# Graph attention's edge pass: source rows gathered per segment instead of per work item

## The reference, cut to what matters

```python
h = (x @ W.T).reshape(n, H, D)                      # one row per node
h_src, h_dst = h[src], h[dst]                       # 200000 edges, sorted by dst
alpha = einsum(h_src, a_src) + einsum(h_dst, a_dst)
alpha = alpha + sum(relu(edge_attr @ edge_W.T + edge_b) * h_dst, -1)
alpha = where(alpha >= 0, alpha, 0.2 * alpha)
ex = exp(alpha - segment_max(alpha, dst)[dst])
attn = ex / segment_sum(ex, dst)[dst]
out = segment_sum(h_src * attn, dst)
```

## Time and profile before

| | us |
|---|---|
| median of 3 runs | 4161.73 (4161.46 to 4166.39) |
| the profiled execution | 4158.91 |
| its span, first to last instruction | 4157.1 |
| PE / DVE / ACT / POOL busy | 3517.1 / 2547.6 / 2043.5 / 2185.5 |

### The profile page before, as it was taken

One profiled execution on the slowest core, in us unless ns is written; L12 is line 12 of the kernel. 1 busy time (PEld: TensorE's weight loads), 2 busy tenths in 40 slices (PEclk: granted clock), 3 DMA queues, 4 the chain that ended last, 5 costly groups with the idle time before them and its releaser, 6 DMA issues.

```text
span 4157.1 us, 87425 instructions
## 1 busy us (share of the span) xinstructions
PE 3517.1 (85%) x22054; PEld 2416.0 (58%) x22055; DVE 2547.6 (61%) x6056; ACT 2043.5 (49%) x5653; POOL 2185.5 (53%) x2124
## 2 busy tenths in 40 slices
PE   4788899958888888888888888888888869919999
PEld 3447788835555555555555555555555547808888
DVE  5657655557777777777777777777777754411121
ACT  2312333326666666666666666666666644503232
POOL 3302000047777777777777777777777711151111
PEclk8899999989999999999999999999999989959999
DMA  4631011145555555555555555555555531021110
GB/s 151 199 124 48 28 35 32 33 100 125 135 134 139 136 134 138 136 139 138 138 136 141 141 141 144 140 140 139 138 143 139 143 140 30 27 63 36 34 39 25
DMA packets 352296, 449.23 MB, mean 108 GB/s; under 512 B 170970, under 2 KB 275163, under 8 KB 350456
## 3 DMA queue, kind: packets, MB, share of 16 engines
q0 software_dynamic: 95568, 267.78, 25.6%
q10 hardware_dynamic: 108338, 124.27, 9.8%
q1 hardware_dynamic: 147943, 52.09, 5.2%
HBM read 389.57 MB, written 55.13 MB: 107 GB/s over the span
## 4 chain that ended last, share of the span: by engine, by line
PE 34%; DMA 17%; issue 13%; SPq 13%; POOL 8%; DVE 7%; ACT 4%; ACTq 3%; POOLq 0%; DVEq 0%
SPq L428 9%; DMA al<-h_tab,idx 6%; DMA al<-pen_d 6%; PE bank L1175 5%; PE bank L1187 5%; PE bank L989 4%; POOL al L521 4%; PE bank L1134 4%; PE bank L998 4%; PE bank L1083 3%; SPq L414 3%; PE bank L1024 2%; DMA gbuf<-h_tab,idx 2%; POOL gbuf L521 2%; PE bank L902 1%
## 5 line engine op out<-in xcount | busy, mean ns | idle before, releaser
L521 POOL DMA_INDIRECT al<-h_tab,idx x976 | 1107.1, 1134 | 309.9 <-issue 279.9
L521 POOL DMA_INDIRECT gbuf<-h_tab,idx x784 | 843.5, 1076 | 400.3 <-issue 379.8
L1024 PE MATMUL bank<-oneh_t,hbt 125*128 125x512 bf16 x2640 | 719.7, 413 | 189.0 <-DVE oneh_t L1442 167.4
L746 ACT ACTIVATE enc<-bank,eb 128x512 f32<-128x512 f32 x880 | 554.7, 682 | 299.6 <-issue 192.5
L1449 DVE SCALAR_TENSOR_TENSOR prod<-enc,adst,bank 128x512 f32<-128x512 f32 x880 | 628.6, 734 | 11.9 <-PE bank L1014 11.9
L1083 PE MATMUL bank<-msg,oneh 128*125 128x264 f32 x2352 | 629.2, 414 | 7.3 <-DVE r L1536 3.9
L1083 PEld LDWEIGHTS bank<-msg,oneh 128*125 128x125 f32 x2352 | 473.2, 205 | 160.4 <-issue 47.3
L1024 PEld LDWEIGHTS bank<-oneh_t,hbt 125*128 x2640 | 245.6, 102 | 529.3 <-issue 353.4
L763 ACT ACTIVATE dist<-iota_n,dtile 128x125 f32<-128x125 f32 x1760 | 552.7, 389 | 0.7 <-PE bank L1083 0.5
L1046 PE MATMUL bank<-prod,hsel 128*32 128x128 f32 x7040 | 283.8, 279 | 58.6 <-issue 58.3
L1536 DVE TENSOR_TENSOR r<-r,bank 125x264 f32 x440 | 187.3, 426 | 221.7 <-PE bank L1014 195.1
(11 more groups left out here) (254 smaller groups left out, 5599.7 us busy)
## 6 DMA issues: line engine op xcount, KB each, us to landing
dstb<-dst ACTq DMA_DIRECT2D x440, 125.0 KB
al<-pen_d SPq DMA_DIRECT2D x1760, 4.0 KB
att<-attrx ACTq DMA_DIRECT2D x880, 24.0 KB
al<-h_tab,idx POOLq DMA_INDIRECT x976
link<-links SPq DMA_DIRECT2D x880, 0.2 KB
gbuf<-h_tab,idx POOLq DMA_INDIRECT x784
attrx<-al ACTq DMA_DIRECT2D x8, 1176.0 KB, 12.3
hsplit<-hb POOLq DMA_DIRECT2D x25, 375.0 KB, 5.5
```

What stands on the lines that cost most here:

```text
L521: pool.indirect_dma_start(slot(n)[:, c, :], None, h_tab, bass.IndirectOffsetOnAxis(ap=idx[g % 2][:, k:k + 1], axis=0)).then_inc(gathered[n ...
L746: m = act.activation(enc[n % 2][:, k, :], bank[k][:, :], ACT.Relu, bias=eb[:, k:k + 1])
L1024: pe.matmul(bank[2 + 2 * q + k][:, :], hbt[:, ds(t & (HT - 1), 1), a, k * 128:(k + 1) * 128].rearrange("p t c -> p (t c)"), oneh_t[q][:, : ...
```

## The change

Gathers are counted by segments. Segment m's rows are gathered once, in order, into slot m mod 16 of a ring that is now one piece of `al`. ACT and DVE find an item's slot with a register that holds its segment: `slot_of(s)`. A new semaphore `rows_in` counts the segments that have landed: POOL raises it for segment m-1 behind the third gather of segment m, after waiting for the landing, and ACT waits for `rows_in` > s. When a slot is free is a third list in `items`, computed once on DVE: for segment m, the larger of (last item of segment m-16) + 17 and (last item of segment m-2) + 1, as a count of `stepped`; POOL loads it into registers, four segments at a time, from segment 16 on. Index loads are one DMA per four segments into 16 index buffers, without registers. DVE loads one more list of registers every four steps, for `m_msg`; ACT keeps the list that it has already. `spare` becomes 0, and the experts' buffers move: `wd` lies in `al`, the tiles that lay in `al` in a new `al2`; ACT waits for `rows_in` = 392 before it loads `wd`. A second small matmul and four small DVE instructions in the setup make the list.

```diff
-        al = sb("al", [128, NCH * H])
-        items = sb("items", [1, 2 * ITP], I32)
+        al = sb("al", [128, RING_END])
+        items = sb("items", [1, 3 * ITP], I32)
...
-        def slot(n):
-
-            b = n % RING
-            if b < RING_B:
-                return gbuf[:, 4 * b:4 * b + 4, :]
-            at0 = (b - RING_B) * 4 * HR
-            return al[:, at0:at0 + 4 * HR].rearrange("p (c w) -> p c w", c=4)
+        gbuf = al[:, NCH * H:RING_END].rearrange("p (c w) -> p c w", w=HR)
+        idx = [sb(f"idx{q}", [128, 4 * G], I32, gather_mem) for q in range(NI)]
+        ring = al[:, RING_AT:RING_END].rearrange("p (j w) -> p j w", w=HR)
+
+        def slot(m):
+
+            b = (m + RING - RING_B) % RING
+            return ring[:, 4 * b:4 * b + 4, :]
+
+        def slot_of(m):
+
+            return ring[:, ds(((m + (RING - RING_B)) & (RING - 1)) * 4, 4), :]
...
@@ SP @@
             def load_idx(g):
-                s = item_regs(sp, 0, G * g)
-                if g >= 2:
-                    for n in range(G * (g - 2), G * (g - 1)):
-                        sp.wait_ge(gathered[n % NGS], 64 * (n // NGS) + 64)
-                for i in range(G):
-                    sp.dma_start(idx[g % 2][:, 4 * i:4 * i + 4], io["src_s"][ds(s[i], 1)].rearrange("s p c -> p (s c)")).then_inc(idx_in[g % 2], 16)
+                wait(sp, rows_in, G * (g - NI) + G)
+                wait(sp, idx_in[g % 2], 16 * (g // 2))
+                sp.dma_start(idx[g % NI][:, :].rearrange("p (s c) -> p s c", c=4), io["src_s"][G * g:G * g + G].rearrange("s p c -> p s c")).then_inc(idx_in[g % 2], 16)
...
             load_idx(1)
+            load_idx(2)
...
-                if g < NG:
-                    load_idx(g)
+                if g + 1 < NSG:
+                    load_idx(g + 1)
...
@@ GpSimd @@
-            def gather(n):
-
-                g = n // G
-                if n % G == 0:
-                    pool.wait_ge(idx_in[g % 2], 64 * (g // 2) + 64)
-                wait(pool, gathered[n % NGS], 64 * (n // NGS))
-                wait(pool, msg_ready, n - RING + 1)
-                wait(pool, stepped, min(n, STEPS) if n >= RING else 0)
+            def rows_landed(m):
+
+                pool.wait_ge(gathered[m % NGS], 64 * (m // NGS) + 64)
+                pool.sem_inc(rows_in, 1)
+
+            def gather(m, after=None):
+
+                g = m // G
+                if m % G == 0:
+                    pool.wait_ge(idx_in[g % 2], 16 * (g // 2) + 16)
+                if after is not None:
+                    pool.wait_ge(stepped, after & 511)
                 pool.sem_inc(went_on, 1)
                 for c in range(4):
-                    k = 4 * (n % G) + c
-                    pool.indirect_dma_start(slot(n)[:, c, :], None, h_tab, bass.IndirectOffsetOnAxis(ap=idx[g % 2][:, k:k + 1], axis=0)).then_inc(gathered[n % NGS], 16)
+                    k = 4 * (m % G) + c
+                    pool.indirect_dma_start(slot(m)[:, c, :], None, h_tab, bass.IndirectOffsetOnAxis(ap=idx[g % NI][:, k:k + 1], axis=0)).then_inc(gathered[m % NGS], 16)
+                    if c == 2 and m > 0:
+                        rows_landed(m - 1)
...
             pool.wait_ge(acc_stored, 16 * SB)
+            pool.wait_ge(tables_stored, 32)
...
-            pool.wait_ge(tables_stored, 32)
-            for n in range(RING_B, RING_B + 4):
-                gather(n)
+            for m in range(RING_B, RING_B + 4):
+                gather(m)
             clear(r1[:, :], 0.0)
-            for n in range(RING_B + 4, ITEMS):
-                gather(n)
+            for m in range(RING_B + 4, RING):
+                gather(m)
+            pool.wait_ge(items_ready, 1)
+            for g in range(RING // G, NSG):
+                free = item_regs(pool, 2, G * g, G)
+                for i in range(G):
+                    gather(G * g + i, free[i])
+            rows_landed(NS - 1)
...
@@ ScalarE @@
-            def keep_asrc(n):
+            def keep_asrc(n, s):
                 i = n % G
-                act.wait_ge(gathered[n % NGS], 64 * (n // NGS) + 64)
-                act.activation(apad[(n // G) % 2].rearrange("p (c i h) -> p c i h", c=4, i=G)[:, :, i, :], slot(n)[:, :, 0:H], ACT.Copy).then_inc(asrc_kept, 1)
+                act.wait_ge(rows_in, (s & 511) + 1)
+                act.activation(apad[(n // G) % 2].rearrange("p (c i h) -> p c i h", c=4, i=G)[:, :, i, :], slot_of(s)[:, :, 0:H], ACT.Copy).then_inc(asrc_kept, 1)
...
@@ VectorE @@
+                    own(v.tensor_scalar(lastm, iota_i[:, :], cnt[:, 0:1], None, ALU.is_ge))
...
+                    own(v.tensor_tensor(lastm[0:1, :], iota_i[0:1, :], bank[2][0:1, 0:ITP], ALU.add))
+                    own(v.tensor_scalar(lastm[0:1, :], lastm[0:1, :], 1.0, None, ALU.add))
+                    own(v.scalar_tensor_tensor(items[0:1, 2 * ITP + RING:2 * ITP + NS], lastm[0:1, 0:NS - RING], float(LM + 2), lastm[0:1, RING - 2:NS - 2], ALU.add, ALU.max))
...
-            def m_msg(n):
+            def m_msg(n, s):
                 g, i = n // G, n % G
                 v.wait_ge(ex_kept, g + 1)
-                v.wait_ge(gathered[n % NGS], 64 * (n // NGS) + 64)
...
+                    if k + G > LM and k - LM < ITEMS:
+                        m0 = max(0, k - LM)
+                        s_msg = item_regs(v, 0, m0)
```

More of the change, by code:

```diff
@@ L53 @@
 RING_B = 7
+RING_AT = NCH * H - (RING - RING_B) * 4 * HR
+RING_END = NCH * H + RING_B * 4 * HR
+NSG = NS // G
+assert NSG * G == NS
+NI = 16
 NGS = 6
@@ L144, in build_program @@
         eb, adst = sb("eb", [128, KC]), sb("adst", [128, KC])
-        dst_s = al[:, NCH * H - EP // 256:].bitcast(I16)
+        dst_s = al[:, NCH * H - EP // 256:NCH * H].bitcast(I16)
         gather_mem = ExitStack()
         dst_f = sb("dst_f", [128, NCH], at=gather_mem)
-        gbuf = sb("gbuf", [128, GBC, HR], at=gather_mem)
-        idx = [sb(f"idx{q}", [128, 4 * G], I32, gather_mem) for q in range(2)]
-        def slot(n):
-            b = n % RING
-            if b < RING_B:
-                return gbuf[:, 4 * b:4 * b + 4, :]
-            at0 = (b - RING_B) * 4 * HR
-            return al[:, at0:at0 + 4 * HR].rearrange("p (c w) -> p c w", c=4)
+        gbuf = al[:, NCH * H:RING_END].rearrange("p (c w) -> p c w", w=HR)
[6 more added lines that the diff above has]
+            return ring[:, ds(((m + (RING - RING_B)) & (RING - 1)) * 4, 4), :]
         consts_in, x_in, wa_in, edges_in, wkv_in = sem("consts_in"), sems("x_in", XC), sem("wa_in"), sem("edges_in"), sem("wkv_in")
@@ L202, in build_program @@
         lastb = early[0:64, 3656:3656 + ITP]
+        lastm = al[0:64, 0:ITP]
         thr = sb("thr", [64, 3], at=mem_a2)
@@ L269, in build_program @@
         acc = r1[0:P, 0:T * HO].rearrange("p (t c) -> p t c", t=T)
-        mem_2 = ExitStack()
-        wd = sb("wd", [128, NE, JF * C], at=mem_2)
         mem_d = ExitStack()
+        al2 = sb("al2", [128, 4864], at=mem_d)
+        xg = [sb(f"xg{u}", [128, SROW], at=mem_d) for u in range(2)]
+        xo = [sb(f"xo{u}", [128, SROW], at=mem_d) for u in range(2)]
+        og = [sb(f"og{u}", [128, C], at=mem_d) for u in range(2)]
+        xa = sb("xa", [P, 2, C], at=mem_d)
+        ag = sb("ag", [P, 2, C], at=mem_d)
+        xst2 = sb("xst2", [P, 2, 6], at=mem_d)
+        mvr = sb("mvr", [P, 2, 2], at=mem_d)
+        dn = sb("dn", [P, 2, 2, H], at=mem_d)
         wgt = sb("wgt", [128, JF, 32], at=mem_d)
@@ L293, in build_program @@
         sidx = sb("sidx", [P, T], I32, mem_d)
-        xg = [sb(f"xg{u}", [128, SROW], at=mem_d) for u in range(2)]
-        xgn = [al[:, 8400 + C * u:8400 + C * (u + 1)] for u in range(2)]
-        xo = [sb(f"xo{u}", [128, SROW], at=mem_d) for u in range(2)]
         oidx = [sb(f"oidx{u}", [128, 1], I32, mem_d) for u in range(2)]
-        og = [sb(f"og{u}", [128, C], at=mem_d) for u in range(2)]
         mem_d.close()
-        mem_2.close()
+        rt = [al[0:P, T * NE * i:T * NE * (i + 1)] for i in range(6)]
+        xgn = [al[:, 2400 + C * u:2400 + C * (u + 1)] for u in range(2)]
+        wd = al[:, RING_END - NE * JF * C:].rearrange("p (e q) -> p e q", e=NE)
         x2 = r1[0:P, 0:T * HO].rearrange("p (t c) -> p t c", t=T)
[L303 to L306, removed]
+        lgs = al2[:, 4608:4608 + W2T]
+        hT = al2[:, 0:JF * 256].rearrange("p (j n) -> p j n", j=JF)
+        xdT = al2[:, 2048:2048 + KC * 256].rearrange("p (k n) -> p k n", k=KC)
+        bdr = al2[:, 2560:2560 + NE * C]
         node_in = sem("node_in")
@@ L354, in item_regs @@
         def item_regs(eng, which, first, count=4):
-            top = [NS - 1, T - 1][which]
+            low, top = [(0, NS - 1), (0, T - 1), (1, STEPS)][which]
             return nc.values_load_multi_w_load_instructions(
-                items[0:1, ds(which * ITP + first, count)], engines=[eng.engine], min_val=0, max_val=top,
+                items[0:1, ds(which * ITP + first, count)], engines=[eng.engine], min_val=low, max_val=top,
```

(3 more changed lines are left out.)

22 lines of the change are left out of this document (9 added, 13 removed).

## The result

The changed kernel takes **4060.68 us** (median of 4 runs, 4057.51 to 4063.27), the kernel before 4161.59 in the same comparison: ratio 0.9759, 95% interval 0.9747 to 0.9771. The prediction said 4075 us, range 3985 to 4170. The profiled execution took 4063.27 us, its span 4061.4.

The account below looks back on a forecast made before the run. POOL's queue of gathers was taken to set the pace, ScalarE next. Early -16, late -84, ring +10, landings +6 and start -4 make -88, from 4158.9 to 4071 us profiled, about 4075 as median; range 3985 to 4170.

Parts of the forecast that it names:

- 1, 2. Gathers and POOL's price: POOL, edge pass: 1568 gathers for 1760; 5.18 us a segment, including 0.15 for register loads, plus 0.65 an item.
- the prediction's rule: POOL's gathers: GpSimd shares its SBUF interface with VectorE, so their stretch, 0.65 us an item, belongs to the 440 messages.
- The two readings of it: POOL's time saved by 192 fewer gathers: 272 us if the stretch is the gathers' own, 241 if the messages'.
- 3. Landings: POOL before a segment's fourth gather: waiting for the previous segment's rows costs 0.05 us a segment, at worst 0.9.
- rival C: Landing waits on POOL of 0.9 us a segment cost 107 us more early on: about 4180 us; chance 0.05.
- 4. The ring: Slot release between POOL, ScalarE and PE: a 17.5 us loop over three steps, without slack, adds +10 us.
- 5. Register work: ScalarE and VectorE: offsets and a third VectorE load cost 0, covered by earlier waits; bare, 0.1 and 0.15 us a step.
- B: Register work lands on the loop of ScalarE and VectorE: 5.74 us a step, +35, about 4197 us; chance 0.14.
- B's second condition: Sign in the edge pass that register work slows the kernel: steps exceed 5.6 us with POOL idle.
- 6. SP: SP's index loads become one DMA per group; VectorE's 197.5 us of penalty waits should go, which cost nothing under full POOL.
- 7. Start: Start of the edge pass: indices come earlier and the slot a step later, -4 us.
- A: ScalarE has more room, so POOL bounds the edge pass throughout: -185, about 4000 us; chance 0.17.

Follow-up runs that it names:

- again_2: Changed kernel with 48 segments gathered twice, so 1760 gathers again: 4763.88 us, 1.0230 of the kernel before on its chip.
- experiment 3: Changed kernel with every ring slot released one step later: 4660.72 and 4630.93 us, 0.9918 and 0.9954 of the kernel before on the same chips.
- sp_alone: Kernel before with four index buffers instead of two, gathers still 1760: 4704.44 us, ratio 1.0005.
- control: Changed kernel unedited, on another chip: 4509.98 us, 0.9689 of the kernel before there.
- ring_msg: Changed kernel with a ring slot released by its last message instead of the later step: 5111.53 us, 1.0890 of the kernel before.
- experiments 4 and 5: Changed kernel with slots released by message: 5111.53 us; register lists aligned to four words on ScalarE 4524.87, VectorE 4505.80, both 4531.93 and 4526.75 us.

## Why the prediction came out right, point by point

**1, 2. Gathers and POOL's price.** 1568 gathers, as counted. The price was too high: 0.946 and 0.30 us as taken, 5.00 for four; but the register load doesn't show in the gaps, whose median is 0.305 us at each of the 16 places of a round, and all "issue" gaps together exceed that by 25 us in 358 segments, so it cost at most 0.07 a segment and not 0.15; and the stretch is (1515.8 - 1434 x 0.946)/404 = 0.39 us an item and not 0.65. It does lie beside the messages, as the prediction's rule has it: of the gathers from 1000 to 3200 us, those during which a message ran took 1.31 us in the mean before (651 of them) and 1.14 after (666), the others 0.97 and 0.99. That an item's share stays the same didn't hold. Why it shrank isn't shown. The two readings of it, 272 and 241 us for 192 gathers, can't be told apart by again_2 (264, give or take 21).

**3. Landings.** Felt 83 times in 2200 us, 46.6 us in all, 0.13 us a segment where I took 0.05. By the Trainium skill (DMA: Bandwidth & Descriptors, Anatomy of one DMA) they would never be felt; the trace decides otherwise, but the amount is small and rival C falls.

**4. The ring.** Right in mechanism: 5.97 us a step for items 31 to 61 against 5.79 before, and by the chain and experiment 3 it is this loop. The +0.18 beside the text's +0.2 is partly luck. The text has the 0.2 on top of POOL's own 5.83, together 6.03; POOL's own need was 5.0 to 5.07 and 0.39, at most 5.46, so the ring added 0.5, and the two errors cancel. From item 56 on repeated segments already loosen it.

**5. Register work.** The cover that I named for VectorE's load, the waits of L1521, went from 79 to 18 times, as B feared, and the load shows as 118.4 us of bare time. Yet steps didn't exceed 5.6: B's second condition failed, and with it B.

**6. SP.** Right: no cost by sp_alone, no waits for penalties after.

**7. Start.** The -4 came: from item 0 to item 16 the pass gained 4.2 us on the kernel before. But the first step starts 2.6 us later, of which 2.3 are already there some 35 us ahead of the pass, at the end of the projections; the text had no term for it. What it comes from isn't shown. At the start two shorter waits for landings replace the one of 9.19 us for indices:

```profile
882.08 0.94 POOL L530 DMA_INDIRECT al<-h_tab,idx  x1 [2.57 <-DMA al<-h_tab,idx]
...
888.82 0.95 POOL L530 DMA_INDIRECT al<-h_tab,idx  x1 [2.05 <-DMA al<-h_tab,idx]
```

**The sum.** By its own terms the prediction has the pass 8 us late at item 80, 4 ahead at item 149 and 88 ahead at the end; measured are 6 late, 14 ahead and 93 ahead, and 96 between the profiled executions. The late pace was forecast as 5.39 and is 5.40 from item 149 on. Part of that is luck: 5.39 was one reading of one round of four steps, the other was 5.27, which over 291 items makes 35 us, and nothing in the text decides between them. The turn from POOL to ScalarE was put at item 149 and lies near item 70: with the measured price POOL needs at most 5.46 us for a segment with one item, so only the ring stood in the way. The term that was off is POOL's price (5.18 + 0.65): from item 80 to 149 steps took 5.34 us where the text's price and landings make them 5.5, 11 us of gain that it doesn't have. Predicted -88, measured -96. A, that POOL would bound to the end, was wrong as argued: POOL idles late, and ScalarE had no more room.

## What to carry to other kernels

Price a removed instruction by the whole loop that it sits in, and then ask at once who is next, with that engine's pace read from the chain, over more rounds than one. Count a ring by how many steps its release loop may span: here a loop of 17 us over two steps instead of three took steps from 6.9 to 8.3 us, and it is felt only where nothing repeats. And try a change on more than one chip before judging it by tenths of a per cent: 2.4% here were 3.1 and 3.2% elsewhere.

## What the runs showed of the hardware that I had not expected

**A register load's time goes by the address.** A list from `items` that begins at a multiple of four words takes 0.31 to 0.35 us on VectorE, TensorE and POOL, and 0.31 on ScalarE behind another load (0.49 for the first of a pair). One that doesn't takes 0.96 us on VectorE and 1.09 to 1.14 on ScalarE. The Trainium skill (DMA: Bandwidth & Descriptors, Latency and other measured facts) puts such a load at about 600 ns at least; the short ones take half of that.

**The same program took 11 to 13% longer on other chips, and TensorE's signal is what is late there.** All but some 20 us of it lie in the edge pass: its steps take 2465 us in the kernel before and 2989 in sp_alone, and what follows them 813 and 815. The mean granted clock and the span of after and of control:

```profile
core 0: 4061.4 us, clock 0.959
```

```profile
core 0: 4511.6 us, clock 0.908
```

In the semaphore events of the pair's traces the step's signal comes 0.02 us in the median behind the modelled end of the matmul that gives it (the second L1036 of a step), and never over 0.3 us, before and after. In control it comes later by 0.45 us in the median, by over 2.65 us at a quarter of the steps, and by 7.0 at most from 1000 to 3200 us; in ring_msg by 0.8 in the median and by over 6 at a quarter. The signals of ScalarE and VectorE, where they are recorded, come 0.01 us behind the end on either chip. All other engines then halt together, as in this piece of control's timeline:

```profile
2008.39 1.47 PE L1046 MATMUL bank<-oneh_t,hbt 125*128 125x512 bf16 x6
...
2012.86 1.26 ACT L763 ACTIVATE enc<-bank,eb 128x512 f32<-128x512 f32 x2 [4.14 <-remote]
2012.97 0.43 DVE L1561 TENSOR_TENSOR r<-r,bank 125x264 f32 x1 [4.46 <-remote]
...
2013.55 1.13 PE L1105 MATMUL bank<-msg,oneh 128*125 128x264 f32 x4 [3.69 <-DVE r L1561]
```

"remote" stands here because half of the semaphore events are missing from these traces. The granted clock falls to the lower of its two levels beside such a halt or right behind it (71 of 74 low stretches in control). In the piece above the six matmuls of L1046 are recorded as begun before the halt, so it is open whether TensorE itself stood still or only its signal came late, and what makes it late is open too. It may be why experiments 4 and 5, which gave other engines room, gave no time.
